# A Mamba-2 block and a mixture-of-experts layer on one core: softplus ahead of both Silus, the decay sums a slot sooner, merged transposes

## The reference

```python
x = x + _L0_attn_ref(_layernorm(x), ...)   # Mamba-2 block, D_INNER 256, 8 heads, state 64
x = x + _L0_ffn_ref(_layernorm(x), ...)    # 2 shared and 4 routed experts of width 512, top 2 of 4

# in the Mamba-2 block
h = rmsnorm(hidden, w_norm_in); proj = h @ w_in_proj        # z, x, B, C, dt_raw
x = silu(causal_conv4(x) + conv_b)
dt = softplus(dt_raw @ w_dt + b_dt); dt_h = dt.reshape(..., 8, 32).mean(-1)
# ssd_scan, in chunks, per head
lcs = cumsum(dt_h * A); M = exp(where(mask, lcs_l - lcs_i, -inf)); G = C @ B.T
y = (M * G) @ x + exp(lcs) * C @ h;  h = exp(lcs[-1]) * h + (M[-1] * x).T @ B
y = rmsnorm((y + x * D) * silu(z), w_norm_out)
return residual + y @ w_out_proj
# in the expert layer
w = softmax(x @ gate_w + gate_b); top 2 kept
shared = mean over 2 of (relu(x @ sw1 + sb1) @ sw2 + sb2)
routed = sum over kept of w_e * (relu(x @ rw1[e] + rb1[e]) @ rw2[e] + rb2[e])
```

## Time and profile before

| | |
|---|---|
| runs, median (lowest, highest) | 577.71 us (575.64, 581.18), 3 runs |
| profiled execution | 576.64 us, span 574.9 us, granted clock 0.996 |
| TensorE busy | 548.7 us (95%), 4016 matmuls |
| VectorE, ScalarE, GpSimd busy | 437.6 (76%), 356.2 (62%), 172.6 us (30%) |
| chain that ended last, by engine | TensorE 48%, VectorE 19%, issue 11%, ScalarE 9%, DMA 5%, GpSimd 5% |
| DMA sizes a body | segments 512 KB each (4), growth rows 128 KB each (6), output store 256 KB |

### The profile page before, as it was taken

One profiled execution on the slowest core, in us unless ns is written; L12 is line 12 of the kernel. 1 busy time (PEld: TensorE's weight loads), 2 busy tenths in 40 slices (PEclk: granted clock), 3 DMA queues, 4 the chain that ended last, 5 costly groups with the idle time before them and its releaser, 6 DMA issues.

```text
span 574.9 us, 11864 instructions
## 1 busy us (share of the span) xinstructions
PE 548.7 (95%) x4016; PEld 429.8 (75%) x4016; DVE 437.6 (76%) x1037; ACT 356.2 (62%) x767; POOL 172.6 (30%) x232
## 2 busy tenths in 40 slices
PE   8886999999999999999999999999999999999996
PEld 7665767877777777877787777777778787777774
DVE  4878767887789785888688786987768787676654
ACT  3894488637675477636795477745787376852442
POOL 2073504521163202631046201622036210542011
PEclk9999999999999999999999999999999999999999
DMA  6650006300550006600272004700064003510120
GB/s 204 183 152 2 0 33 190 84 1 2 147 173 3 1 6 175 143 1 0 81 173 65 0 0 155 164 0 0 15 198 106 0 1 105 157 44 1 38 59 21
DMA packets 37354, 41.43 MB, mean 72 GB/s; under 512 B 3482, under 2 KB 27716, under 8 KB 37316
## 3 DMA queue, kind: packets, MB, share of 16 engines
q1 hardware_dynamic: 36724, 40.80, 25.9%
q10 hardware_dynamic: 592, 0.15, 0.1%
HBM read 37.79 MB, written 3.15 MB: 71 GB/s over the span
## 4 chain that ended last, share of the span: by engine, by line
PE 48%; DVE 19%; issue 11%; ACT 9%; DMA 5%; POOL 5%; SPq 1%; DVEq 0%; ACTq 0%; POOLq 0%
PE bank L424 7%; PE bank L426 5%; PE bank L425 5%; PE bank L535 4%; PE bank L642 4%; PE bank L644 4%; PE bank L643 4%; DVE act_l L1268 4%; DVE cv L1121 4%; DMA grow<-lc_rows 3%; ACT act_h L874 3%; PE bank L547 2%; PE bank L563 2%; PE bank L435 2%; ACT L967 2%
## 5 line engine op out<-in xcount | busy, mean ns | idle before, releaser
L1268 DVE SCALAR_TENSOR_TENSOR act_l<-bank,act_h 128x512 fp32r<-128x512 f32 x192 | 131.3, 686 | 69.8 <-ACT act_h L874 68.6
L874 ACT ACTIVATE act_h<-bank 128x512 fp32r<-128x512 f32 x192 | 114.1, 594 | 81.9 <-PE bank L426 78.0
L424 PE MATMUL bank<-fTl,w1h 128*128 128x512 f32 x192 | 86.9, 452 | 3.0 <-DVE fTl L1219 2.3
L1492 POOL TENSOR_TENSOR late<-late 128x512 f32<-128x512 f32 x31 | 39.8, 1285 | 163.3 <-DVE late L1276 163.3
L894 ACT ACTIVATE seg<-seg,lneg 128x128 f32<-128x128 f32 x256 | 81.2, 391 | 2.8 <-DMA seg<-lc_rows 2.8
L642 PE MATMUL bank<-act_l,w2h 128*128 128x512 f32 x192 | 77.5, 404 | 1.6 <-DVE act_l L1268 1.5
L425 PE MATMUL bank<-fTh,w1l 128*128 128x512 f32 x192 | 75.7, 394 | 0.0
L644 PE MATMUL bank<-act_h,w2h 128*128 128x512 f32 x192 | 75.6, 394 | 0.0
L426 PE MATMUL bank<-fTh,w1h 128*128 128x512 f32 x192 | 75.6, 394 | 0.0
L643 PE MATMUL bank<-act_h,w2l 128*128 128x512 f32 x192 | 75.2, 392 | 0.0
L1479 POOL TENSOR_TENSOR xw<-xs,seg 128x128 f32<-128x128 f32 x48 | 19.9, 414 | 157.3 <-ACT seg L894 82.8
(11 more groups left out here) (176 smaller groups left out, 1063.6 us busy)
## 6 DMA issues: line engine op xcount, KB each, us to landing
seg<-lc_rows SPq DMA_DIRECT2D x32, 512.0 KB, 4.5
late<-gk_rows SPq DMA_DIRECT2D x8, 1024.0 KB, 9.3
grow<-lc_rows SPq DMA_DIRECT2D x48, 128.0 KB, 5.4
x_in<-L_attn_hidden_dram SPq DMA_DIRECT2D x8, 256.0 KB, 3.7
out_dram<-late SPq DMA_DIRECT2D x8, 256.0 KB, 2.5
late<-L_ffn_sw_dram SPq DMA_DIRECT2D x2, 512.0 KB, 7.2
late<-L_ffn_rw_dram SPq DMA_DIRECT2D x1, 1024.0 KB, 7.7
CT<-L_attn_w_in_proj_dram SPq DMA_DIRECT2D x1, 512.0 KB, 5.3
```

The lines of the kernel that those rows point to most:

```text
L424: mm(dst, stat_h, mov_l, start=True, stop=False)
L874: nc.scalar.activation(act_h[:, b % RING, :], HID[b % 2][:], ACT.Relu).then_inc(act_h_ready, 1)
L1268: v_.scalar_tensor_tensor(act_l[:, r, :], HID[b % 2][:], 0.0, f(act_h[:, r, :]), ALU.max, ALU.subtract)\
```

## The change

- `lcs` and `g_transposes` have one full-width instruction group each in place of four narrow ones. For it `dta` and `kept` get 32 columns a chunk, of which the excess is zeroed once, in the opening.
- TensorE: both `x_tokens` are in slot 6; `lcs` is in slot 7 behind `proj` 10 and 11.
- ScalarE: `softplus` is in slot 3, under the table set that is already loaded, with the load of the Silu set right behind it; `silu_z` 0, two B copies and `silu_x` 0 are in slot 4 ahead of the Relu, `silu_x` 1, `silu_z` 1 and the other load behind it; B copy 3 is ahead of the Relu of slot 6, both `xs_copy` behind it; `chunk_decays` is in slot 7.
- VectorE: `dt_add` 0 is ahead of `norm2_apply`; `dt_clamp` is in slot 1; one tap in slot 2 and three in slot 3, behind that slot's `act_low`; `dt_decay` is in slot 5; `store` is behind `act_low` in its slot.
- SyncE: `segments` 0 is issued ahead of the output store.

The opening's order is as before, but for what `lcs` issues.

```diff
-        dta = sb("dta", [P, (NCH - 1) * NH + 32])
+        dta = sb("dta", [P, NCH, 32])
-        kept = sb("kept", [P, (NCH - 1) * NE + 32])
+        kept = sb("kept", [P, NCH, 32])
...
# sync, body
-                if older is not None:
-                    sp_eng.wait_ge(out_ready, nth(older, 1, 1))
-                    sp_eng.dma_start(out_dram[older], out_t).then_inc(out_stored, 16)
...
                     sp_eng.wait_ge(lc_written, nth(s, 16, 16))
                     segments(s, 0)
+                if older is not None:
+                    sp_eng.wait_ge(out_ready, nth(older, 1, 1))
+                    sp_eng.dma_start(out_dram[older], out_t).then_inc(out_stored, 16)
+                if s is not None:
                     segments(s, 1)
...
# tensor, lcs
-                mm(sums[:, 0:32], upto[:], dta[:, 0:32], start=True, stop=True)
-                for c in range(NCH):
-                    ins = mm(sums[32 * c:32 * c + 32, P:2 * P], dta[:, c * NH:c * NH + 32], upto[:], start=True, stop=True)
-                ins.then_inc(lcs_psum, 1)
+                mm(sums[:, 0:32], upto[:], dta[:, :, 0:NH], start=True, stop=True)
+                mm(sums[:, P:2 * P], dta[:].rearrange("p c q -> p (c q)"), upto[:], start=True, stop=True).then_inc(lcs_psum, 1)
# tensor, g_transposes
-                for c in range(NCH):
-                    ins = mm(MAIN[2][32 * c:32 * c + 32, 0:P], kept[:, c * NE:c * NE + 32], ident[:], start=True, stop=True)
-                ins.then_inc(gT_psum, 1)
+                nc.tensor.transpose(MAIN[2][:, 0:P], kept[:].rearrange("p c q -> p (c q)"), ident[:]).then_inc(gT_psum, 1)
# tensor, scan_part
                 if i in (5, 6):
                     proj(s, i + 3)
-                    x_tokens(s, i - 5)
+                if i == 6:
+                    x_tokens(s, 0)
+                    x_tokens(s, 1)
                 if i == 7:
                     proj(s, 10)
                     proj(s, 11)
+                    lcs(s)
                 if i == 8:
-                    lcs(s)
                     proj(s, 13)
# scalar, scan_part
-                if i == 2:
+                if i == 3:
+                    softplus(s)
                     nc.scalar.preload_act_table_set("silu_and_others")
-                if i == 3:
+                if i == 4:
                     silu_z(s, 0)
-                    silu_x(s, 0)
-                if i == 4:
-                    silu_z(s, 1)
                     b_copy(s, 0)
                     b_copy(s, 1)
-                    silu_x(s, 1)
+                    silu_x(s, 0)
                 if i == 7:
                     c_copy(s, 1)
+                    chunk_decays(s)
                 if i == 8:
-                    chunk_decays(s)
                     c_copy(s, 3)
# scalar, body
+                    if s is not None and i == 6:
+                        b_copy(s, 3)
                     if new := block_at(i, prev, older):
                         relu(*new)
-                    if s is not None and i in (5, 6):
-                        b_copy(s, i - 3)
-                        xs_copy(s, i - 5)
+                    if s is not None and i == 4:
+                        silu_x(s, 1)
+                        silu_z(s, 1)
+                        nc.scalar.preload_act_table_set("natural_log_exp_and_others")
+                    if s is not None and i == 5:
+                        b_copy(s, 2)
+                    if s is not None and i == 6:
+                        xs_copy(s, 0)
+                        xs_copy(s, 1)
...
-                    if s is not None and i == 4:
-                        nc.scalar.preload_act_table_set("natural_log_exp_and_others")
-                        softplus(s)
# vector, scan_part
-                if i == 6:
+                if i == 5:
                     dt_decay(s)
# vector, body
-                    if older is not None and i == (7 if s is not None or prev is None else 9):
-                        store(older)
...
                         act_low(*new)
+                    if older is not None and i == (7 if s is not None or prev is None else 9):
+                        store(older)
...
+                    if s is not None and i == 1:
+                        dt_add(s, 0)
                     if prev is not None and i == 1:
                         norm2_apply(prev)
...
                         if i == 1:
-                            dt_add(s, 0)
                             dt_add(s, 1)
+                            dt_clamp(s)
                         if i == 2:
-                            conv(s, 1, (0, 1))
+                            conv(s, 1, (0,))
                         if i == 3:
-                            conv(s, 1, (2, 3))
-                            dt_clamp(s)
+                            conv(s, 1, (1, 2, 3))
```

More of the change, by code:

```diff
@@ L1138, in dt_decay @@
                 dve.wait_ge(dt_steps, nth(s, 3, 2))
-                v_.tensor_tensor(dta[:, 0:NCH * NH].rearrange("p (c h) -> p c h", h=NH), dsum[:].rearrange("p (c h) -> p c h", h=NH),
+                v_.tensor_tensor(dta[:, :, 0:NH], dsum[:].rearrange("p (c h) -> p c h", h=NH),
                                  a_neg[:].unsqueeze(1).to_broadcast([P, NCH, NH]), ALU.mult).then_inc(dt_steps, 1)
@@ L1254, in top_two @@
                 step(8)
-                v_.scalar_tensor_tensor(kept[:, 0:NCH * NE], rank[:], 1.5, gw_n[:].rearrange("p c e -> p (c e)"),
+                v_.scalar_tensor_tensor(kept[:, :, 0:NE], rank[:].rearrange("p (c e) -> p c e", e=NE), 1.5, gw_n[:],
                                         ALU.is_lt, ALU.mult).then_inc(gate_kept, 1)
@@ L1431, in opening @@
                                 channel_multiplier=1).then_inc(tables_set, 1)
-                for t, v in ((ones[:], 1.0), (upto[:], 1.0), (turn[:], 0.0), (lower[:], 1.0), (center[:], -1.0 / P), (dta[:, NCH * NH:], 0.0), (kept[:, NCH * NE:], 0.0)):
+                for t, v in ((ones[:], 1.0), (upto[:], 1.0), (turn[:], 0.0), (lower[:], 1.0), (center[:], -1.0 / P), (dta[:, :, NH:], 0.0), (kept[:, :, NE:], 0.0)):
                     g.memset(t, v).then_inc(zeros_set, 1)
```

## The result

The changed kernel took 583.73 us (583.03 to 586.33, 4 runs), the kernel before, beside it, 577.60 us (575.64 to 581.18, 4 runs): ratio 1.0118, interval 1.0083 to 1.0153. The forecast was 575.9, the range 570.5 to 582.5. The profiled execution took 586.33 us (span 584.6, granted clock 0.988) and lies 2 to 3 us above its three neighbours: its opening ran 3.4 us longer than before, which no step of the change explains. TensorE in order of time (start, duration, what) shows one place: sixteen passes of filler matmuls (`keep_busy_early`, which multiplies the identity by itself) in 3.78 us. The profile before (at 7.95) and those of all twelve experiments have 2.05 for the same sixteen.

The account below looks back on a forecast made before the run. TensorE, busy 95%, was taken as the bound. Six bodies -0.3, body 1 +0.3, the transposes-only body -0.4, opening -0.15, DMA -1.2: -1.75 from 576.64 gives 574.9; the median stands 1.07 above: 575.9 us, range 570.5 to 582.5.

Parts of the forecast that it names:

- block 2, second layer of block 0: 210.35: TensorE walk of a middle body, after projection 9 and the x transposes: these end at 210.35, with no wait.
- Rival B: VectorE's queue delays the older sequence's last term and so the output transposes: +6 to +7, 582.5 us; chance 0.14.
- Silu z half 1 and projection 9: Slot 4: projection 9 needs bank 1 from Silu z half 1, starts at 207.4, a new wait of 1.35 us.
- rival A: Projection 9's new wait does not come: 565 us, chance 0.10; halfway, a wait of 0.7: 571.5 us, chance 0.13.
- D: Rival: table load costs as much again ahead of Relu 23, chain to projection 9 1.3 later: 585 us; chance 0.03.
- Merged groups: TensorE: full-width instead of narrow matmuls gain 0.4 us at the kept-weights transposes and 0.13 at the decay sums.
- E: Rival: the narrow groups were nearly free, array term 0 in all eight bodies and the opening: 580 us; chance 0.03.
- The new position of the store costs nothing: SyncE's queue: segment 0 goes ahead of the output store, which nobody needs before slot 12; no cost.
- The DMA term: Segment 0 issued sooner on SyncE shortens TensorE's mg waits: 1.2 us taken, between 0 and 1.7.
- C: Rival: the sums sooner do nothing, growth rows stay behind the store, mg waits remain: 577.1 us; chance 0.10.
- One body: Middle body: 0.35 us later up to projection 13, with 0.4 from the transposes 0.05 us shorter; six bodies.
- Body 1: Body without older blocks: fTl 0.55 later, waits of 0.75 and 1.5 at projections 8 and 9; +0.7 less 0.4.

Follow-up runs that it names:

- e2: Changed kernel with the older sequence's last term moved ahead of the decay steps and logits on VectorE: 575.54 us.
- e5: Changed kernel with the older sequence's last term first, Silu of z half 1 first, and the narrow matmul groups restored: 572.53 us.
- e7: Changed kernel with the output store ahead of segment 0 again, as before: 586.62 us.
- e3: Changed kernel with the Silu of z half 1 ahead of the Silu of x half 1 in slot 4: 587.11 us.
- e9: Changed kernel with last term first, Silu of z half 1 first, and Relu 23 ahead of softplus and its table load: 570.28 us.
- e10: Changed kernel with last term first, Silu of z half 1 first, and segment 1 and growth rows also ahead of the output store: 568.28 us.
- e6: Changed kernel, in body 1 alone with the first dt addition back behind the normalisation and weight split: 581.38 us.
- e1: Kernel before with only the merged full-width matmuls (decay sums and kept-weights transposes): 580.00 us.
- e11: Kernel before with the merged matmuls, and the output store behind segments 0 and 1 and the growth rows: 571.41 us.

## Why the prediction was wrong, step by step

- **The failed step** is "block 2, second layer of block 0: 210.35". It has no wait in it. By my own walk the layer was due at 210.35 - 0.70 = 209.65, and the term that must leave its bank was "ready 210.8": a wait of 1.15, times six bodies 6.9 us, which makes the forecast 582.8. I held the term only against its other reader, the output transposes, and took its old place (206.93) as harmless. Measured 1.02 to 1.12, and e2, which removes that wait alone, takes the loss away. Of the 7.8 us between forecast and median it is 7.1 with the slower step behind each; body 1 (below) is 1.9 more, and the smaller terms take about 1 off.
- Rival B had the mechanism, VectorE's queue reaching TensorE through the older sequence's last term, but at a reader that the walk had 2.5 us later (212.2 instead of 209.65), and so as a case that needs 0.8 us of extra delay. It needed none.
- Silu z half 1 and projection 9: forecast 1.35 from one start to the other, measured 1.44 to 1.47 (1.28 to 1.31 of it idle) in six bodies; projection 8's 0.36 measured 0.41 from its due start (0.27 idle). The ScalarE walk was right: rival A fell, and D too: 0.03 us from Ln's end to the load, 0.01 from the load to Relu 23. The Trainium skill, ScalarE: Activation LUTs, What ACT_TABLE_LOAD costs, counts about 1.283 us for the load and a drain of some 1.38 beside it. The trace agrees on the load, 1.28, and shows no drain.
- Merged groups: mis-sized a little. From the last matmul ahead of the kept transposes to the second behind them it was 1.02 us (217.92 to 218.94) and is 0.57: gain 0.45 (forecast 0.4). The sums take 0.44 start to start instead of 0.59, gain 0.15 (forecast 0.13), or 0.26 with the slow first step behind the narrow group (0.34, where 0.23 is usual). Together 0.60 to 0.71 instead of 0.53; e5 gives 0.53 a body. E fell. Of the 0.45 at the kept weights most is the group itself: its eight passes took 0.35 from start to next start, the one transpose 0.03; the steps ahead of it (0.33) and behind it (0.34) are 0.1 over the usual 0.23 each, the step behind the transpose (0.31) 0.08. The Trainium skill, TensorEngine Tiling (Array Packing), Theoretical Speedup, has up to 4 times for such groups. Here, at the sums, eight narrow passes took 0.36 us and the two full ones in their place 0.30, so the four tiles gained nothing.
- "The new position of the store costs nothing" held, and was too small a view: the store's place is worth 3.1 us of `mg` waits (e7). The DMA term, 1.2, measured 1.7. C fell.
- One body: -0.05, + 1.12 for the wait, + 0.1 for the slower step behind it, - 0.07 to 0.18 for the groups, - 0.1 for the output transposes that did not wait, + 0.17 for projection 9 starting at 213.64 instead of 213.47: 1.06 to 1.17. Measured 1.09 and 1.04, bodies 5 and 6.
- Body 1: forecast +0.3, measured +2.2. The wait was nearly as walked (1.62 idle, where the earlier trace rows have 1.0 at the longest and I had 0.55 more); the clock that fell behind it was in no term. The other profiles show its price. From the weight fold to the mark body 1 takes 26.6 us before and 28.8 in the changed kernel, e2 and e7, where the clock falls in it. It takes 27.0 in e3, e9 and e10, where `fTl` makes TensorE wait 1.6 us too and the clock stays full (these three have the Silu of z first): +0.4, close to the forecast. "Full in every slice" was read from the page's digits, where 9 covers anything from 0.9: the same profile of before, asked for 55 to 60 us, has 0.67.

```profile
55.00:60.00 5.00, 5.00 (x26) 4.30 (x24) 1.59 (x6) 0.54 (x2) 1.01 (x1) 0.67 0.00 0
```

What stays open: why the clock falls in body 1 or the opening in some executions and not in others. e10's profile has it full in body 1 behind a wait for `fTl` as long as the changed kernel's (1.6 us), e6's falls there behind a shorter one. Open too is why sixteen filler passes took 3.78 us in one execution.

## What to carry to other kernels

When an instruction moves later on its engine, list **every** semaphore that it raises and every bank or buffer that it frees, and set its new time against each reader and each overwriter; the first one due decides, not the one that uses the result. Of two waits on one chain the sooner pays only once the later is gone, and the later one must be looked for before the sooner is priced. In a list of DMA issues that one engine works through in order, a store that nobody waits for belongs behind the loads that somebody waits for: here, with the merged groups in place, that was worth 8.6 us (e1 to e11).

## What the runs showed of the chip that I had not expected

- TensorE's clock fell to 1.2 of its 2.4 GHz behind single waits of 1.6 to 2.2 us in a kernel that is 95% busy; in the kernel before too, behind the 2.2 us at the end of its opening, and in e6 behind 1.04. In e2's body 1 a stretch lies wholly at the lower level (granted clock 0.50):

```profile
75.00:80.00 5.00, 4.91 (x15) 3.53 (x14) 4.33 (x8) 4.97 (x9) 0.00 (x0) 0.50 0.00 0
```

  In e3, behind one of six like waits of 2.0 to 2.1 us (start, duration, what; then stretches of the same execution, granted clock 0.71 and 0.79):

```profile
279.77 0.50 PE L639 MATMUL bank<-act_l,w2h 128*128 128x512 f32 x1 [2.09 <-DVE late L1278]
...
281.24 0.63 PE L426 MATMUL bank<-hTh,wl 128*128 128x512 f32 x1
281.67 0.63 PE L427 MATMUL bank<-hTh,wh 128*128 128x512 f32 x1
```

```profile
279.00:282.00 3.00, 2.23 (x6) 1.82 (x7) 1.91 (x3) 1.13 (x4) 1.29 (x1) 0.71 0.00 0
282.00:286.00 4.00, 4.00 (x19) 3.36 (x19) 2.39 (x11) 1.55 (x4) 0.00 (x0) 0.79 0.06 16
```

  The same wait in body 3 of that execution, at 212.47, left the clock alone. Where it fell, in three of the six, the body took 68.5 to 68.8 us instead of the 67.0 to 67.3 of the changed kernel: a wait of 2 us can cost 1.5 to 1.6 more behind it. That the wait is the cause is read from the order of events; no run isolated it, and a wait of that length alone does not decide it.
